# Inverse roots by one POOL power in place of nine DVE operations

## The reference

```python
# token block: h is the 64-wide row of a token
mu = jnp.mean(h, axis=-1, keepdims=True)
var = jnp.mean(jnp.square(h - mu), axis=-1, keepdims=True)
h = (h - mu) * jax.lax.rsqrt(var + LN_EPS) * gamma + beta
h = jax.nn.silu(h)
...
def _layernorm(x, axis=-1, eps=1e-05):
    m = jnp.mean(x, axis=axis, keepdims=True)
    v = jnp.var(x, axis=axis, keepdims=True)
    return (x - m) / jnp.sqrt(v + eps)
...
kv_ret = kv_ret / (jnp.sqrt(gate_cum) * sqrtP)
combined = mh_out + kv_ret
lnx = (combined - mu) / jnp.sqrt(var + 1e-05) * ln_g + ln_b
return x + (lnx @ out_w + out_b)
...
h = h + attn(_layernorm(h), ...)
h = h + ffn(_layernorm(h), ...)
```

## Time and profile before

| | us |
|---|---|
| median of 3 runs | 214.59 (214.52 to 216.08) |
| profiled execution | 213.43 |
| its span on the core | 211.7 |
| PE busy | 147.7 (70% of the span) |
| DVE busy | 131.1 (62%) |
| ACT busy | 73.9 (35%) |
| POOL busy | 35.6 (17%) |
| granted TensorE clock, mean | 0.778 |

### The profile page before, as it was taken

How to read it: one execution, slowest core, us unless ns; L and a number is a source line. 1 busy time by engine, 2 the same in 40 slices (tenths; PEclk the granted TensorE clock), 3 DMA queues, 4 the chain that set the end, 5 groups by cost and what they waited for, 6 DMA issues and landing times.

```text
span 211.7 us, 2099 instructions
## 1 busy us (share of the span) xinstructions
PE 147.7 (70%) x690; PEld 90.8 (43%) x690; DVE 131.1 (62%) x342; ACT 73.9 (35%) x122; POOL 35.6 (17%) x52
## 2 busy tenths in 40 slices
PE   0889858029279694499581054877479989979992
PEld 0543524024175512458561053766454454534340
DVE  2659995789942898998879995388673005101011
ACT  2010511252233640784840230323063462444541
POOL 2031500346000472241402330000000000000000
PEclk9999979758857955558997555799555896799998
DMA  5999600000000000000000000000000000101011
GB/s 145 345 386 377 262 5 25 0 0 0 0 0 0 0 0 0 0 5 2 0 0 5 0 0 0 0 5 0 0 0 0 0 3 0 25 0 25 0 25 25
DMA packets 7042, 8.80 MB, mean 42 GB/s; under 512 B 2388, under 2 KB 4436, under 8 KB 7032
## 3 DMA queue, kind: packets, MB, share of 16 engines
q1 hardware_dynamic: 7032, 8.68, 12.2%
HBM read 8.15 MB, written 0.52 MB: 41 GB/s over the span
## 4 chain that ended last, share of the span: by engine, by line
PE 43%; DVE 34%; issue 9%; DMA 5%; ACT 5%; POOL 2%; SPq 1%; DVEq 0%; POOLq 0%; ACTq 0%
PE bank L900 8%; PE bank L884 6%; DMA dist_sb<-in_dist 5%; PE bank L885 4%; PE bank L861 2%; PE bank L640 2%; DVE dist_sb L988 2%; PE bank L705 2%; PE bank L698 2%; PE bank L702 2%; DVE proj L1059 2%; PE bank L707 2%; DVE invpos L993 2%; PE bank L690 2%; PE bank L754 1%
## 5 line engine op out<-in xcount | busy, mean ns | idle before, releaser
L586 ACT ACTIVATE hid<-bank 128x512 f32<-128x512 f32 x32 | 18.1, 596 | 23.3 <-PE bank L885 22.2
L900 PE MATMUL bank<-hid,ffn_sb 128*64 128x512 f32 x64 | 18.9, 676 | 0.0
L1271 DVE TENSOR_TENSOR h<-bank,h 128x256 f32<-128x256 f32 x4 | 1.7, 425 | 27.0 <-PE bank L909 27.0
L884 PE MATMUL bank<-xp,w1hi 128*128 128x512 f32 x32 | 16.6, 520 | 1.0 <-ACT xp L570 1.0
L885 PE MATMUL bank<-xp,w1lo 96*128 96x512 f32 x32 | 14.6, 455 | 0.0
L884 PEld LDWEIGHTS bank<-xp,w1hi 128*128 128x128 f32 x32 | 7.0, 220 | 14.4 <-ACT hid L586 8.1
L988 DVE TENSOR_TENSOR dist_sb<-dist_sb,mask_in 128x1024 f32<-128x1024 f32 x8 | 9.5, 1232 | 4.0 <-POOL mask_in L325 4.0
L698 PE MATMUL bank<-late_sb,proj 128*128 128x8 f32 x16 | 3.7, 364 | 10.8 <-ACT proj L469 10.8
L656 PE MATMUL bank<-early_sb,vk 128*128 128x128 f32 x8 | 2.2, 435 | 12.9 <-DVE vk L1038 12.9
L830 PE MATMUL bank<-early_sb,sq_c 128*128 128x2 f32 x16 | 2.9, 304 | 11.8 <-ACT sq_c L545 11.8
L640 PE MATMUL bank<-dist_sb,neigh 128*64 128x512 f32 x32 | 11.1, 775 | 0.0
(11 more groups left out here) (246 smaller groups left out, 369.4 us busy)
## 6 DMA issues: line engine op xcount, KB each, us to landing
dist_sb<-in_dist SPq DMA_DIRECT2D x4, 1024.0 KB, 10.8
mask_in<-in_mask SPq DMA_DIRECT2D x4, 256.0 KB, 10.0
ffn_sb<-in_ffn SPq DMA_DIRECT2D x1, 813.0 KB, 10.9
fold_sb<-in_folded SPq DMA_DIRECT2D x1, 772.0 KB, 12.1
late_sb<-in_late SPq DMA_DIRECT2D x1, 728.5 KB, 11.6
out<-h SPq DMA_DIRECT2D x8, 64.0 KB, 1.7
early_sb<-in_early SPq DMA_DIRECT2D x1, 391.0 KB, 3.2
mask_in<-in_mrows SPq DMA_DIRECT2D x1, 128.0 KB, 2.4
```

Of the source, the lines that this page charges most:

```text
L586: nc.scalar.activation(hid[:, at % HB], bank[hid_bank[at % 3]][:, :], ACT.Gelu).then_inc(S["hid_set"], 1)
L884: nc.tensor.matmul(o, w1hi[:, e * HID:(e + 1) * HID], xp1[g][:, toks], start=True, stop=False)
L900: mm = nc.tensor.matmul(bank[2][j * D:(j + 1) * D, :], K["e_w2"][:, (e + j) * D:(e + j + 1) * D], hid[:, (at + j) % HB], start=False, stop ...
```

## The change

Each of the five kinds of root becomes one operation on POOL, `tensor_tensor` with the operation pow, whose second input is a tile filled with -0.5. The helper `rsqrt` and three scratch tiles go. DVE hands the input over by a semaphore, POOL writes the result, and DVE waits for it. The powers stand in POOL's queue at the entry of ORDER where DVE's root stood. Core of the diff (declarations of the semaphores left out):

```diff
+        minus_half = sb("minus_half", [P, 40])
-        rs_a = sb("rs_a", [P, 40])
-        rs_u = sb("rs_u", [P, 40])
-        rs_y = sb("rs_y", [P, 40])
 def _(pool):
     nc.gpsimd.memset(ones[:, :], 1.0).then_inc(S["ones_set"], 1)
+    nc.gpsimd.memset(minus_half[:, :], -0.5).then_inc(S["power_set"], 1)
...
+    pool.wait_ge(S["power_set"], 1)
+
+    def power(dst, src, done):
+        nc.gpsimd.tensor_tensor(dst, src, minus_half[:, 0:src.shape[1]], ALU.pow).then_inc(S[done], 1)
 def token(g):      # POOL, after the selects
     yield
-    yield
-    yield
-    yield
+    pool.wait_ge(S["h1_var"], g + 1)
+    power(st_r[:, :], rs_v[:, 0:8], "h1_rstd")
+    yield
+    yield
+    yield
+    pool.wait_ge(S["x_var"], g + 1)
+    power(st_r[:, :], rs_v[:, 0:8], "x_rstd")
     if g == 0:
...
 def queries(g):    # POOL, after L369
     yield
     yield
+    pool.wait_ge(S["q_var"], 2 * g + 2)
+    power(rs_w[:, :], rs_q[:, :], "q_rstd")
     yield
     pool.wait_ge(S["k_feat"], 2 * g + 1)
...
 def chunks(g):     # POOL
-    for _ in range(9):
+    for _ in range(7):
         yield
+    pool.wait_ge(S["var_read"], g + 1)
+    power(st_c[:, :], rs_v[:, 0:8], "c_rstd")
+    yield
+    yield
 def weights(g):    # POOL
     pool.wait_ge(S["kang_set"], 8)
+    pool.wait_ge(S["h1_rstd"], NG)
 def experts(g):    # POOL
     yield
-    yield
-    yield
-    yield
-    for _ in range(20):
+    pool.wait_ge(S["x2_var"], g + 1)
+    power(st_r[:, :], rs_v[:, 0:8], "x2_rstd")
+    for _ in range(23):
         yield
...
-            def rsqrt(out_ap, n, source=rs_v):
...             (the nine DVE operations)
 def variance(squares, done):   # DVE
-    link(nc.vector.tensor_reduce(rs_v[:, 0:8], squares[:, :, :], AX_X, ALU.add))
+    nc.vector.tensor_reduce(rs_v[:, 0:8], squares[:, :, :], AX_X, ALU.add).then_inc(S[done], 1)
 def token(g):      # DVE; the x and x2 roots likewise
     dve.wait_ge(S["h1_sq"], g + 1)
-    variance(sq)
-    rsqrt(st_r[:, :], 8)
+    variance(sq, "h1_var")
+    dve.wait_ge(S["h1_rstd"], g + 1)
 def queries(g):    # DVE
-    link(nc.vector.tensor_scalar(rs_q[:, 32:40], gsum[:, g], 1.0, float(PH), ALU.max, ALU.mult))
-    yield
-    rsqrt(rs_w[:, :], 40, rs_q)
+    nc.vector.tensor_scalar(rs_q[:, 32:40], gsum[:, g], 1.0, float(PH), ALU.max, ALU.mult).then_inc(S["q_var"], 1)
+    yield
+    dve.wait_ge(S["q_rstd"], g + 1)
 def chunks(g):     # DVE
     nc.vector.tensor_scalar(rs_v[:, 0:8], bank[4][:, 0:8], EPS, None, ALU.add).then_inc(S["var_read"], 1)
-    dve.wait_ge(S["var_read"], g + 1)
-    rsqrt(st_c[:, :], 8)
     yield
+    dve.wait_ge(S["c_rstd"], g + 1)
     dve.wait_ge(S["attn_mm"], g + 1)
```

More of the change, by code:

```diff
@@ L240, in tower @@
         dve_step, pool_step = sem("dve_step"), sem("pool_step")
-        names = """ones_set w1_centred tables_mm tables_set ids_set spread_mm onehot_set neigh_mm neigh_set diag_off
+        names = """power_set h1_var h1_rstd x_var x_rstd q_var q_rstd c_rstd x2_var x2_rstd ones_set w1_centred tables_mm tables_set ids_set spread_mm onehot_set neigh_mm neigh_set diag_off
             dist_masked h1_mm h1_copied h1t_mm h1_sq h1_norm hn_mm f_set h2_mm h_set x_centred x_sq x_set
@@ L937, in magnitude, with variance @@
                 return nc.vector.tensor_scalar(dst.bitcast(I32), src.bitcast(I32), 0x7FFFFFFF, None, ALU.bitwise_and)
-            def rsqrt(out_ap, n, source=rs_v):
[L941 to L954, removed]
-                link(nc.vector.tensor_reduce(rs_v[:, 0:8], squares[:, :, :], AX_X, ALU.add))
+            def variance(squares, done):
+                nc.vector.tensor_reduce(rs_v[:, 0:8], squares[:, :, :], AX_X, ALU.add).then_inc(S[done], 1)
             def centre(dst, src, done):
@@ L1048, in token @@
                 dve.wait_ge(S["x_sq"], g + 1)
-                variance(sq)
-                rsqrt(st_r[:, :], 8)
+                variance(sq, "x_var")
+                dve.wait_ge(S["x_rstd"], g + 1)
                 nc.vector.tensor_tensor(v8(x[:, g]), v8(hc[:]), bc(st_r[:, :], D), ALU.mult).then_inc(S["x_set"], 1)
@@ L1114, in queries @@
                 link(nc.vector.tensor_tensor(wscr[:, 0], wscr[:, 0], wscr[:, 1], ALU.add))
-                nc.vector.tensor_scalar(rs_q[:, 0:32], wscr[:, 0], 1e-30, None, ALU.max)
-                link(nc.vector.tensor_scalar(rs_q[:, 32:40], gsum[:, g], 1.0, float(PH), ALU.max, ALU.mult))
+                nc.vector.tensor_scalar(rs_q[:, 0:32], wscr[:, 0], 1e-30, None, ALU.max).then_inc(S["q_var"], 1)
+                nc.vector.tensor_scalar(rs_q[:, 32:40], gsum[:, g], 1.0, float(PH), ALU.max, ALU.mult).then_inc(S["q_var"], 1)
                 yield
-                rsqrt(rs_w[:, :], 40, rs_q)
+                dve.wait_ge(S["q_rstd"], g + 1)
                 nc.vector.tensor_copy(gcr[:, g], rs_w[:, 32:40]).then_inc(S["gcr_set"], 1)
@@ L1236, in experts @@
                 dve.wait_ge(S["x2_sq"], g + 1)
-                variance(sq)
-                rsqrt(st_r[:, :], 8)
+                variance(sq, "x2_var")
+                dve.wait_ge(S["x2_rstd"], g + 1)
                 link(nc.vector.tensor_tensor(v8(x2[:]), v8(x2[:]), bc(st_r[:, :], D), ALU.mult))
```

## The result

The changed kernel takes 225.97 us (225.89 to 226.41, 4 runs), the kernel before 214.56 (213.88 to 216.08, 4 runs). The ratio is 1.0526, with a 95% interval from 1.0468 to 1.0583: slower by 5.3%, 11.4 us. The profiled execution took 226.0 us, its span is 224.3. So the time lies above the whole range of the forecast, beyond rival 2's 222.2.

The account below looks back on a forecast made before the run. Neither PE nor DVE alone bound it: a relay between engines before 157 us, TensorE after. Gains 1.12 + 1.02 + 0 + 0.10 + 1.30 + 1.12 + 0.57 = 5.23 us gave 209.4 from the 214.59 median; range 206.5 to 221.5, likeliest 207.8 to 212.5.

Parts of the forecast that it names:

- rival 2: Between L1116 and L1119, both groups: the 40-column power is dear; at 150 ns a column 222.2 us; slower, chance 0.27.
- D: 40-column root of group 0: scan and product gain 1.94 us, additions return behind the power; gain 1.50 - p, 0.10 us.
- handovers: DVE to POOL and back at each root: 0.14 us each way, 0.28 together.
- E: 40-column root of group 1: power runs beside DVE's masking of a chunk, gcr starts at 112.52; gain 1.30 us.
- C: h1 root of group 1: POOL and DVE alternate strictly behind it, L409 is released by ACT; gain 0.
- A: h1 root of group 0: L1038 starts 1.12 us earlier, batch 3's selects hidden by 0.2 us; gain 1.12 us.
- B: x root of group 0: 2.03 us becomes 0.72, L1051 may wait 0.29 for one copy; gain 1.02 us.
- F: Combined variance root of group 0, before L1216, which also needs PE L835: gain 1.12 us, at most 1.3.
- G: x2 root of group 0, before PE L855: PE's own L835 ends late, so about 0.57 of 1.12 us passes.
- Rivals 1, 4 and 5: Besides rival 1 and Rival 5, code loading: the first power pays a load once, in A; 214.6 us, chance 0.03.
- rival 1: All powers on POOL as cheap as an add: 7.73 us gained, so 206.9 us; chance 0.12.
- Rival 5: A, B and G swallowed by masks, copies and alternation; D, E and F stay, 2.5 us: 212.1 us, chance 0.07.

Follow-up runs that it names:

- e2: Changed kernel with only the 8-column roots on POOL, the two 40-column roots back on DVE: 213.88 us against 213.82 for the kernel before, ratio 1.0008.
- e1b: Changed kernel with every power replaced by a POOL multiplication of the same shape, inverse root left out: 205.61 us against 214.16 for the kernel before, ratio 0.9525.
- e3: Changed kernel with only the two 40-column roots on POOL, the eight narrow ones back on DVE: 226.06 us against 213.82 for the kernel before, ratio 1.0547.
- e6: Kernel before with ten powers and two multiplications of differing width, exponent and input added on POOL in the experts' stage: 231.93 us.
- e9: Kernel before with POOL's residual additions moved out of DVE's way and two weight differences behind them: 208.60 us against 214.50, ratio 0.9723.
- e10: Kernel before with the added POOL operations of e6 plus five powers, some on 1 or 4 partitions; no kernel time given.

## Why the prediction was wrong

- **The price of a power** is the step that failed. "I take c = 30 ns": by the durations of 8 and 40 columns it is 160. The bounds were 1.67 and 150, so even the upper one was too low, and the value chosen from them was too low by more than five times. The 20 steps at 1 to 2 ns a column were an argument and no row: the columns' price of an addition says nothing of one that computes a power. The fixed part, 0.20, is 0.36. What POOL does in 160 ns a column no run shows.
- **Rival 2, the dear power**, is what happened, with its place (between L1116 and L1119, both groups) and its mechanism. Its formula with the measured p = 6.77 gives D = 1.50 - 6.77 = -5.27 and, by the measured handovers, E = 113.82 - (110.84 + 6.77 + 0.12) = -3.91. The profiles have -5.09 (7.11 less 2.02) and -3.91. It had a chance of 0.27 where the rows could not tell 30 from 150. It ended at 222.2 because its price stopped at 6.20 us, and because the sum had no term for C's queue, the products L640 and the chunk stage (0.75, 1.21 and 1.86 in these two profiles).
- **The handovers**: 0.28 forecast, 0.12 measured. On six roots on the path that is 1.0 us too pessimistic; with the 0.28 of the forecast a narrow root would have cost 1.92 us, more than the nine steps' 1.84, and not 1.77 (e2 comes out even, 1.0008).
- **A, first root, with the masks of batch 3 behind it**: gain 1.12 forecast, 0.07 measured by the price. The cover of 0.2 us was not there: the profile's page gives L654 0.2 us of idle time behind the mask L987, where the kernel before has none. The price isn't to blame for that: with multiplications of 0.20 us (e1b) this wait is 0.5 us. So even a cheap root would have passed on less than 1.12.
- **B**: 2.03 to 1.78, as the copies L339 now run behind the power. The wait of L1051 for one copy was 0.06 (0.75 against 0.69), not 0.29.
- **C**: gain 0 forecast, 0.75 lost. The queue reads copies, third power, L405, L409; that power ends at 46.71, L409 starts at 47.40 and DVE's L1226 takes 3.36 us beside it, not 2.60. e2 has this delay and e3, without the narrow powers, hasn't. The prediction checked this place only for a cheap power.
- **D**, right but for the price: the scan's stage gained 1.83 (1.94 forecast), and the alternation from the power's end to at_arg took 4.23 us (4.45 forecast; at_arg ends at 92.22, the power at 87.99).
- **E, F, G**: mechanism right, price wrong. The roots off the path add nothing that the table shows, as forecast, also at 1.77 us.
- **Rivals 1, 4 and 5**: no first-use load is seen (the first power starts 0.09 us behind the reduction and takes 1.65 us like the others). e1b is rival 1, with 8.3 to 12.0 us for the 7.7 worked out, so the map of what is on the path was right to within a few microseconds in sum; its places were not all right (A, C). Rival 5, with 2.5 us, fell with it.
- **The page's rule in rival 2.** The power of 40 columns takes 6.77 us where DVE's nine steps took 2.07. The GPSIMD Engine Reference of the Trainium skill, section Performance versus the Vector engine, was read for its ratio for an addition, 1.96, and with that ratio it seemed to allow the change. No run here bears that out for a power: a ratio of one operation isn't that of another.

## What to carry over

Where a change swaps many cheap instructions for one that the trace has never shown, the forecast is that instruction's price and nothing else: give the wide range the same care as the sum, and measure the instruction by itself on an idle engine first, as run e6 did with one profile. On POOL a power costs 0.36 us and 0.160 us for each column in the runs here, whatever the partitions, exponent or input; it breaks even here with nine linked DVE steps at 8 columns and loses three times over at 40. Look for POOL operations that read SBUF beside DVE's path: moving four additions and two subtractions, work untouched, took 2.8% off (e9), some 5.9 us, where the forecast hoped for 5.2 from all ten roots.

## What the runs showed that was not expected

- A POOL power takes 1.64 us for 8 columns and 6.77 for 40, where a multiplication of the same shape takes 0.20 and 0.27. One partition costs as much as 128.
- A POOL power does not hold DVE's two-input operations and casts (0.69 and 0.43 us during powers of 2.9 us in e6 and 6.8 us in e10), while an addition, shown with 1.26 us, holds even a copy of 8 columns (1.22 instead of 0.17).
- The same chunk stage runs, from one version to the next, in 11.5 or in 13.5 us, with PE at 0.94 or 0.52 of its clock in the middle of it, and the presence of powers doesn't decide which.
